# A conv-attention-MoE kernel on one core: twelve pipeline passes written out instead of looped, Newton steps of both norms on GpSimd, and x loaded earlier

## The chip, the cores and the metric

One core of a Trainium2 chip runs the whole kernel. The time is the device time in microseconds; a run of the kernel before takes 2311.79 us (median of three). In the profile PE is TensorE's matmul, PEld its weight load, DVE is VectorE, ACT is ScalarE, POOL is GpSimd and SP is SyncE, which only issues transfers.

## The reference, cut to what matters

The input x is (16, 16, 48, 128): 16 batches of 768 tokens with 128 channels. Three layers follow one another, each added to its input:

```
x = x + attention0(groupnorm(x))        # 8 heads of 16, relative biases, causal in t
t = tokens(x)
t = t + additive_attention(layernorm(t))  # logits[i,j] = sum_h w2[h] * tanh(A[i,h] + B[j,h] + b1[h])
t = t + moe(layernorm(t))               # 8 experts, top 2 of a softmax gate, capacity 1920, gelu
```

Both layernorms and the groupnorm are (v - mean) / sqrt(var + 1e-5). The additive attention needs 768 x 768 x 16 values of tanh per batch, the largest single piece of work on ACT.

## The kernel before, in words

**Passes, stages, ticks.** The first two layers and the gate run as a software pipeline over the batches. A pass has 24 ticks; in it five batches are worked on at once, each in another stage: "pre" (groupnorm, q, k, v), "max" (the maxima of the scores), "mid" (scores, softmax, heads, projection, first layernorm, the maps A, B and V), "add" (the additive attention, one group of sums and Tanh per tick) and "end" (the last block of that attention, second layernorm, gate, routing, sending the rows to the experts). Pass b has batch b+3 in "pre", b+2 in "max", b+1 in "mid", b in "add" and b-1 in "end". The first passes come in parts (the list `head`, up to pass 0), passes 1 to 12 are full and run in a loop on the engines (six iterations of two passes), passes 13 to 16 are the tail, and the experts follow (from about 2040 us on). Head and tail passes are written out in the program already.

**Order of work.** Each engine has its own program, made by the same Python function `body(ps)`; it walks over the ticks, and each tick has four slots on PE and DVE (`tick_order`). PE fills three PSUM banks in turn (`ring`), DVE reads them in the same order; PE's fill number n waits for DVE's read n-2. The table `AT` says in which tick a use of the ring stands. In the loop the counts that the waits ask for are worked out from the loop's register. Written-out passes have constants.

**Engines in one pass.** In each tick POOL writes three sums A + B into `hidden` (L837, one slot of four), ACT takes their Tanh (L956, a long one; L962, a fourth group with the sum in its bias), and PE adds them to the logits (L1037). POOL's sums of tick q wait for the logits of tick q-4. ACT also takes the Exp of the scores (L933) and, every fourth tick, of the logits (L940), which waits for a maximum that DVE takes (L1496). DVE takes the maxima of the first layer's scores (L1310) and copies most results out of the ring. POOL sends the rows to the experts too (L866).

**What the change touches.** On SP, `store_block` writes a finished block of `x2` to the output; `load_x` brings the next batch of "pre" into `x_in`, at tick 0 of a pass; the transposes xT of it stand at ticks 1 and 2. The store of block 4 of a pass is the last thing SP does in that pass. On DVE, `norm_scale(which, k)` works out 1/sqrt(var + eps) by a seed (L1194, k = 0) and three Newton steps (L1197, L1199, L1201, with a drain between operations). The second norm (which = 1) carries in its seventh column the groupnorm of the batch in "pre"; its four parts stand at `NORM_AT`, ticks 4 to 6. Its users are the normed rows of "end" (`normed`, L1266, tick 6, slots 1 and 3) and xnT (L1508, tick 7, slot 1). The first norm (which = 0) has only its seed on DVE; its steps run on POOL at tick 20 (L847 to L853). The products B, A and V of the transposed x1 (ticks 21 and 22, L1129 and L1111) wait for the copies of both halves of it.

## Time and profile before

| | before |
|---|---|
| median of 3 runs | 2311.79 us (2310.83 to 2315.6) |
| the profiled execution | 2323.02 us, its span 2321.2 us, mean granted clock 0.969 |
| busy | PE 2069.1 us (89%), ACT 1684.1 us (73%), DVE 1601.4 us (69%), POOL 1519.7 us (65%) |
| instructions with a place in the program | 59625 |

Instructions of a sequencer (register arithmetic, branches, waits, the issue of a transfer) don't count as busy. A row of a timeline gives start and length in us, engine, line, operation, tiles and count, and in brackets how long the engine had been idle and what released it. A pass is placed here from the long Tanh (L956) of its tick 0 to that of the next pass; pass 0 begins at 169.5 us, pass 1 at 274.1 us, pass 13 at 1717.7 us.

### The profile page before, as it was taken

Reading aid. Unit: us, or ns where it says so; the run is one execution under the profiler, and the core shown is the slowest. Engines: PE = TensorE matmul, PEld = TensorE weight load, DVE = VectorE, ACT = ScalarE, POOL = GpSimd, SP = SyncE. Lnnn points to the kernel's source line nnn. Section 1 sums busy time; section 2 is a strip of 40 time slices with the busy share of each in tenths; the row PEclk is TensorE's granted clock in tenths of the full one; section 3 lists DMA queues with packets and bytes.
Section 4 is the critical chain, followed back from the end, with each engine's and each line's share of the span. In section 5 each row is a group of like instructions: output and inputs, shape, how many; then the busy total and the mean of one; then the engine's idle time right before and its main releaser. Section 6 shows DMA issues by size and latency. Waiting matters only on the chain.

```text
span 2321.2 us, 59625 instructions
## 1 busy us (share of the span) xinstructions
PE 2069.1 (89%) x19525; PEld 1205.1 (52%) x19525; DVE 1601.4 (69%) x4309; ACT 1684.1 (73%) x1934; POOL 1519.7 (65%) x1735
## 2 busy tenths in 40 slices
PE   3889999999999999989998989999999978889996
PEld 2555555555554545455554545454555443458775
DVE  7787786868777777778786878686867554424443
ACT  4449887878887888878787888787888988624332
POOL 5117667576766667666767575757576878737777
PEclk7899999999999999999999999999999998999998
DMA  3746321322222323232323232313131000025553
GB/s 97 123 83 145 82 47 56 57 55 52 64 54 65 56 62 58 62 59 61 57 60 61 56 62 48 68 26 77 33 70 30 12 6 5 25 47 86 88 86 36
DMA packets 157506, 138.14 MB, mean 60 GB/s; under 512 B 24665, under 2 KB 149814, under 8 KB 157104
## 3 DMA queue, kind: packets, MB, share of 16 engines
q1 hardware_dynamic: 119376, 109.87, 22.9%
q0 software_dynamic: 23824, 16.85, 5.3%
q10 hardware_dynamic: 13968, 7.30, 1.3%
q8 instruction: 165, 2.70, 0.5%
q14 instruction: 173, 1.42, 0.2%
HBM read 82.68 MB, written 54.52 MB: 59 GB/s over the span
## 4 chain that ended last, share of the span: by engine, by line
PE 42%; DVE 18%; issue 13%; DVEq 9%; POOL 7%; POOLq 4%; ACT 3%; DMA 3%; SPq 2%; ACTq 0%
PE logits L1037 12%; POOL out_dram L590 4%; PE av_bank L1023 4%; PE ring L1137 4%; DVE max_halves L1310 4%; PE ring L1115 4%; PE scores L1007 3%; PE scores L1010 3%; PE ring L1129 3%; POOLq L836 2%; POOL hidden L837 2%; ACT hidden L956 2%; SPq L604 2%; PE ring L1134 1%; PE ring L1100 1%
## 5 line engine op out<-in xcount | busy, mean ns | idle before, releaser
L837 POOL TENSOR_SCALAR hidden<-b_rep,a_cols 128x768 f32<-128x768 f32 x1152 | 1054.9, 920 | 524.0 <-PE logits L1037 292.3
L956 ACT ACTIVATE hidden<-hidden 128x2304 f32<-128x2304 f32 x384 | 816.2, 2126 | 12.1 <-POOL hidden L837 12.1
L1037 PE MATMUL logits<-hidden,w_shifted 128*32 128x384 f32 x6144 | 586.5, 500 | 60.2 <-ACT probs L940 25.4
L933 ACT ACTIVATE probs<-scores 128x512 f32<-128x512 f32 (+1 forms) x768 | 394.4, 547 | 277.5 <-PE scores L1010 274.9
L1310 DVE TENSOR_REDUCE max_halves<-ring 128x4 f32<-128x512 f32 (+1 forms) x704 | 451.0, 659 | 117.6 <-PE ring L1115 117.2
L962 ACT ACTIVATE hidden<-b_rep,a_cols 128x768 f32<-128x768 f32 x384 | 358.5, 934 | 0.0
L1037 PEld LDWEIGHTS logits<-hidden,w_shifted 128*32 128x32 f32 x6144 | 163.2, 110 | 294.3 <-issue 237.7
L1115 PE MATMUL ring<-k_max,q_max 112*128 112x128 bf16 x2688 | 272.0, 224 | 15.4 <-DVE max_halves L1310 11.6
L1007 PE MATMUL scores<-bias_q,onehot_k 112*128 112x512 bf16 (+1 forms) x768 | 275.8, 360 | 4.1 <-DMA q_parts<-max_parts 2.2
L1010 PE MATMUL scores<-q_parts,k_parts 98*128 98x256 bf16 (+1 forms) x1536 | 277.1, 262 | 0.0
L1115 PEld LDWEIGHTS ring<-k_max,q_max 112*128 112x128 bf16 x2688 | 182.1, 99 | 157.4 <-issue 57.3
L866 POOL DMA_INDIRECT expert_rows<-rows,slots x198 | 201.7, 1019 | 59.2 <-issue 37.7
L1023 PE MATMUL av_bank<-probs,v_aug 128*32 128x256 f32 (+1 forms) x3072 | 223.0, 362 | 11.5 <-DVE headsT_raw L1482 10.5
L1010 PEld LDWEIGHTS scores<-q_parts,k_parts 98*128 98x128 bf16 x1536 | 153.1, 100 | 89.9 <-issue 18.5
L940 ACT ACTIVATE probs<-logits,logit_bias 128x768 f32<-128x768 f32 x96 | 86.6, 902 | 107.7 <-DVE logit_bias L1498 105.9
L517 ACT ACTIVATE hidden<-scores,eb1T 128x384 f32<-128x384 f32 x80 | 46.5, 581 | 162.8 <-PE scores L478 160.1
L1137 PE MATMUL ring<-v,probs1T 128*128 128x128 f32 x1152 | 151.2, 282 | 10.9 <-DVE max_halves L1310 9.2
L1137 PEld LDWEIGHTS ring<-v,probs1T 128*128 128x128 f32 x1152 | 138.9, 194 | 24.1 <-DVE max_halves L1310 18.5
L1368 DVE COPY probs1T<-ring 128x384 f32<-128x384 f32 x192 | 101.7, 550 | 43.7 <-PE ring L1134 43.6
L1007 PEld LDWEIGHTS scores<-bias_q,onehot_k 112*128 112x128 bf16 x768 | 78.0, 102 | 96.0 <-issue 65.4
L489 PEld LDWEIGHTS logits<-probs,hidden 128*128 128x128 f32 x960 | 113.4, 192 | 12.5 <-issue 2.2
L1023 PEld LDWEIGHTS av_bank<-probs,v_aug 128*32 128x32 f32 x3072 | 70.0, 108 | 87.7 <-issue 56.0
(272 smaller groups left out, 2665.1 us busy)
## 6 DMA issues: line engine op xcount, KB each, us to landing
qk_parts<-qk_parts_sb SPq DMA_DIRECT2D x16, 1152.0 KB, 4.5
q_parts<-qk_parts SPq DMA_DIRECT2D x192, 96.0 KB, 3.1
k_parts<-qk_parts SPq DMA_DIRECT2D x192, 96.0 KB, 4.1
q_max<-qk_parts SPq DMA_DIRECT2D x96, 96.0 KB
k_max<-qk_parts SPq DMA_DIRECT2D x96, 96.0 KB
expert_rows<-clear_row ACTq DMA_DIRECT2D x9, 792.0 KB, 5.4
x_in<-in_x_dram SPq DMA_DIRECT2D x96, 64.0 KB
x<-in_x_dram SPq DMA_DIRECT2D x96, 64.0 KB
```

Of the source, the lines that this page charges most:

```text
L837: last = g.tensor_scalar(hidden[:, q % SLOTS, o, :], b_rep[:, side], 1.0, a_cols[:, side, a_col(q, o):a_col(q, o) + 1], ALU.mult, ALU.add)
L866: pool.indirect_dma_start(rows_dram, bass.IndirectOffsetOnAxis(slots[:, k, tb:tb + 1], 0), rows[:, tb, :], None, bounds_check=E * CAP - 1, ...
L933: s.activation(probs0[:, d % 3, 2 * pair:2 * pair + 2, 0:n_], scores[:, pair].rearrange("p (j l) -> p j l", j=2)[:, :, 0:n_], ACT.Exp) \
L956: s.activation(hidden[:, t % SLOTS, 0:3, :], hidden[:, t % SLOTS, 0:3, :], ACT.Tanh)
L962: s.activation(hidden[:, t % SLOTS, 3, :], b_rep[:, side], ACT.Tanh, bias=a_cols[:, side, col:col + 1]).then_inc(tanh_done, 1)
L1007: mm(bank[:, :, 0:n_], onehot_k[:], bias_q[:, h:h + 2, q0 - P * kb:q0 - P * kb + n_], start=True, stop=False, skip_group_check=True)
L1010: last = mm(bank[:, j, 0:n_], k_parts[0:98, h + j, P * kb:P * kb + P], q_parts[0:98, h + j, q0:q0 + n_], start=False, stop=True, skip_grou ...
L1023: last = mm(av_bank[32 * g:32 * g + 32, q0 - lo:q0 - lo + n_], v_aug[:, side, kb, 4 * quad + g, :], probs0[:, d % 3, g, 0:n_], start=(kb = ...
L1037: last = mm(logits[32 * g:32 * g + 32, half, 0:HALF], w2_shifted[:, k, :], hidden[:, q % SLOTS, g, HALF * half:HALF * half + HALF], start= ...
L1115: last = mm(bank[:, P * j:P * j + P], q_max[:, h + j, P * qb:P * qb + P], k_max[:, h + j, P * kb:P * kb + P], start=True, stop=True)
L1137: last = mm(bank[:, 0:P], probs1T[:, P * kb:P * kb + P], v1[:, ps.side(stage), kb, :], start=(kb == 0), stop=(kb == TB - 1))
L1310: v.tensor_reduce(max_halves[:, h % 4:h % 4 + n_, BLOCK_PAIRS.index((qb, kb))], bank[:, 0:n_ * P].rearrange("p (h k) -> p h k", h=n_), AX. ...
```

## The change

The loop over passes 1 to 12 becomes twelve copies of the body, with constants in every wait and address. The Newton steps of the second norm move to POOL at tick 6, as those of the first were at tick 20: DVE makes the seed at tick 4 and signals, POOL does twelve small operations and signals back, DVE waits for that before the normed rows (now slots 2 and 3 of tick 6) and before xnT. Where a pass has "pre" and no "mid", the steps stay on DVE. On SP the store of block 4 goes from the end of its pass to tick 1 of the next, behind the load of x. The first half of A, B and V waits for the copy of the first half of x1T alone.

```
@@ -101,7 +101,7 @@
 SPLIT_AT = ((14, 1), (16, 0))
 SEND_FROM, SENDS = 18, 12
 NORM_AT = ((4, 3), (5, 0), (5, 2), (6, 0))
-SCALE_AT = 20
+SCALE_AT = (20, 6)
 SPLIT = 18
 CLEAR_AT = tuple(range(1, 19, 2))
 CLEARS = 1 + len(CLEAR_AT)
@@ -195,10 +195,8 @@
             body(Pass(b, b % 2, stages, base, base % RING, ticks))
             if i == 0 and prepare:
                 prepare()
-        with eng.Fori(0, (last_full - first_full + 1) // 2) as two:
-            for odd in (1, 0):
-                done = two * 2 + (1 - odd)
-                body(Pass(done + first_full, odd, STAGES, done * per_pass + base_full, base_full % RING))
+        for done in range(last_full - first_full + 1):
+            body(Pass(done + first_full, (done + 1) % 2, STAGES, done * per_pass + base_full, base_full % RING))
         base = base_full + (last_full - first_full + 1) * per_pass
         for b in range(last_full + 1, NB + 1):
             body(Pass(b, b % 2, stages_of(b), base, base % RING))
@@ -338,8 +336,8 @@
         av_copied = sem("av_copied")
         res_loaded = sem("res_loaded")
         x1n_ready = sem("x1n_ready")
-        x1_seeded = sem("x1_seeded")
-        x1_scaled = sem("x1_scaled")
+        norm_seeded = [sem(f"norm_seeded_{which}") for which in range(2)]
+        norm_scaled = [sem(f"norm_scaled_{which}") for which in range(2)]
         ab_ready = sem("ab_ready")
         sums_ready = sem("sums_ready")
         tanh_done = sem("tanh_done")
@@ -636,10 +634,10 @@
                 sp.dma_start(k_max[48:96, :, :], ct_wide).then_inc(copies_in, 16)
                 sp.dma_start(k_max[96:112, :, :], cn_wide).then_inc(copies_in, 16)
 
-            def store_block(ps, stage, s):
+            def store_block(ps, stage, s, read):
                 b = ps.batch(stage)
 
-                sp.wait_ge(ring_read, ps.number((stage, "attended", s)) + 1)
+                sp.wait_ge(ring_read, read)
                 sp.sem_inc(sp_passed, 1)
 
                 if positive(count := b * 96 + 16 * s):
@@ -709,17 +707,15 @@
                                 load_max(c, 0)
                         if t == SPLIT and positive(c):
                             load_max(c, 0)
-                    if ps.has("end") and t == 4:
-                        store_block(ps, "end", 5)
+                    if ps.has("end") and t in (1, 4):
+                        store_block(ps, "end", 4 + t // 4, ps.base if t == 1 else ps.number(("end", "attended", 5)) + 1)
                     if ps.has("mid") and t == 7:
                         c = ps.batch("mid")
                         for tb in range(TB):
                             sp.dma_start(x1[:, ps.side("mid"), tb, :], x[c, :, 8 * tb:8 * tb + 8, :]) \
                               .then_inc(res_loaded, 16)
                     if ps.has("add") and t >= 8 and t % 4 == 0:
-                        store_block(ps, "add", t // 4 - 2)
-                if ps.has("add"):
-                    store_block(ps, "add", 4)
+                        store_block(ps, "add", t // 4 - 2, ps.number(("add", "attended", t // 4 - 2)) + 1)
 
             passes(sp, body)
             expert_loads(sp)
@@ -838,10 +834,10 @@
                                            a_cols[:, side, a_col(q, o):a_col(q, o) + 1], ALU.mult, ALU.add)
                 last.then_inc(sums_ready, 1)
 
-            def norm_scale(ps):
-
-                var, y, tmp = (ln_small[:, 0, r, 0:TB] for r in range(3))
-                pool.wait_ge(x1_seeded, ps.batch("mid") + 1)
+            def norm_scale(which, c):
+
+                var, y, tmp = (ln_small[:, which, r, 0:TB + which] for r in range(3))
+                pool.wait_ge(norm_seeded[which], c + 1)
                 pool.sem_inc(pool_passed, 1)
                 for step in range(3):
                     g.tensor_tensor(tmp, y, y, ALU.mult)
@@ -852,7 +848,7 @@
                     pool.drain()
                     last = g.tensor_tensor(y, y, tmp, ALU.mult)
                     if step == 2:
-                        last.then_inc(x1_scaled, 1)
+                        last.then_inc(norm_scaled[which], 1)
                     else:
                         pool.drain()
 
@@ -870,8 +866,10 @@
                 for t in ps.ticks:
                     if ps.has("add"):
                         sums(ps, t)
-                    if t == SCALE_AT and ps.has("mid"):
-                        norm_scale(ps)
+                    if t == SCALE_AT[0] and ps.has("mid"):
+                        norm_scale(0, ps.batch("mid"))
+                    if t == SCALE_AT[1] and (ps.has("mid") or ps.has("end")):
+                        norm_scale(1, ps.batch("pre") - 2)
                     if ps.has("end"):
                         here = sends(ps)
                         if t < TICKS - SEND_FROM:
@@ -1078,7 +1076,7 @@
                 elif name == "x1T":
                     pe.wait_ge(x1n_ready, c + 1)
                 elif name in ("A", "B", "V"):
-                    after("x1T", 1)
+                    after("x1T", i)
                 elif name == "probsT":
                     pe.wait_ge(probs1_ready, c * 6 + (i[0] + 1))
                 elif name == "attended":
@@ -1190,17 +1188,6 @@
         def _(dve):
             v = nc.vector
 
-            def rsqrt_seed(y, var):
-                return v.tensor_scalar(y.bitcast(I32), var.bitcast(I32), -0.5, float(0x5F3759DF), ALU.mult, ALU.add)
-
-            def rsqrt_step(y, var, tmp):
-                v.scalar_tensor_tensor(tmp, y, -0.5, y, ALU.mult, ALU.mult)
-                dve.drain()
-                v.tensor_tensor(tmp, tmp, var, ALU.mult)
-                dve.drain()
-                v.scalar_tensor_tensor(y, tmp, 1.5, y, ALU.add, ALU.mult)
-
-
             def signal():
                 dve.drain()
                 v.memset(flag[:, 1:2], 0.0).then_inc(setup_dve, 1)
@@ -1249,18 +1236,28 @@
                 dve.drain()
                 v.bn_aggr(ln_mv[:, which, tb, :], ln_stats[:, which, tb, :])
 
-            def norm_scale(which, k):
-                n_ = TB + which
-                var, y, tmp = (ln_small[:, which, r, 0:n_] for r in range(3))
-                dve.drain()
+            def rsqrt_seed(which):
+                var, y = (ln_small[:, which, r, 0:TB + which] for r in range(2))
+                dve.drain()
+                v.tensor_scalar(var[:, 0:TB], ln_mv[:, which, :, 1], 1e-5, None, ALU.add)
+                dve.drain()
+                return v.tensor_scalar(y.bitcast(I32), var.bitcast(I32), -0.5, float(0x5F3759DF), ALU.mult, ALU.add)
+
+            def norm_seed(which):
+                rsqrt_seed(which).then_inc(norm_seeded[which], 1)
+
+            def norm_step(which, k):
+
                 if k == 0:
-                    v.tensor_scalar(var[:, 0:TB], ln_mv[:, which, :, 1], 1e-5, None, ALU.add)
-                    dve.drain()
-                    last = rsqrt_seed(y, var)
-                    if which == 0:
-                        last.then_inc(x1_seeded, 1)
-                else:
-                    rsqrt_step(y, var, tmp)
+                    rsqrt_seed(which)
+                    return
+                var, y, tmp = (ln_small[:, which, r, 0:TB + which] for r in range(3))
+                dve.drain()
+                v.scalar_tensor_tensor(tmp, y, -0.5, y, ALU.mult, ALU.mult)
+                dve.drain()
+                v.tensor_tensor(tmp, tmp, var, ALU.mult)
+                dve.drain()
+                v.scalar_tensor_tensor(y, tmp, 1.5, y, ALU.add, ALU.mult)
 
             def normed(which, src, dst, tb):
                 return v.tensor_scalar(dst[:, tb, 0:P], src[:, tb, :], ln_mv[:, which, tb, 0:1],
@@ -1497,23 +1494,26 @@
                             dve.drain()
                             v.tensor_scalar(logit_bias[:, 1:2], logit_bias[:, 0:1], b2_col[:], b2_col[:], ALU.subtract,
                                             ALU.add).then_inc(max1_ready, 1)
-                        if ps.has("pre") or ps.has("end"):
-                            if (t, slot) in NORM_AT:
-                                norm_scale(1, NORM_AT.index((t, slot)))
+                        if (ps.has("mid") or ps.has("end")) and t == 4 and slot == 3:
+                            norm_seed(1)
+                        elif ps.has("pre") and not ps.has("mid") and (t, slot) in NORM_AT:
+                            norm_step(1, NORM_AT.index((t, slot)))
                         for w, (at, first) in enumerate(SPLIT_AT):
                             if ps.has("pre") and t == at and first <= slot < first + 3:
                                 split(w, slot - first, ps.batch("pre"))
                         if ps.has("pre") and t == 7 and slot == 1:
                             dve.drain()
+                            if ps.has("mid"):
+                                dve.wait_ge(norm_scaled[1], ps.batch("pre") - 1)
                             v.tensor_scalar(xnT[:], xT[:], gn_small[:, 0:1], ln_small[:, 1, 1, TB:TB + 1], ALU.subtract,
                                             ALU.mult).then_inc(xn_ready, 1)
                         if ps.has("end"):
                             c = ps.batch("end")
-                            if t == 6 and slot in (1, 3):
-                                if slot == 1:
-                                    dve.drain()
+                            if t == 6 and slot in (2, 3):
+                                if slot == 2:
+                                    dve.wait_ge(norm_scaled[1], ps.batch("pre") - 1)
                                     dve.wait_ge(rows_sent, 112 + c * 192)
-                                for tb in range(3 * (slot // 2), 3 * (slot // 2) + 3):
+                                for tb in range(3 * (slot - 2), 3 * (slot - 2) + 3):
                                     last = normed(1, x2, rows, tb)
                                 if slot == 3:
                                     last.then_inc(x2n_ready, 1)
@@ -1545,11 +1545,11 @@
                                 for tb in range(half.start, half.stop):
                                     v.bn_aggr(ln_mv[:, 0, tb, :], ln_stats[:, 0, tb, :])
                             if t == 17 and slot == 2:
-                                norm_scale(0, 0)
+                                norm_seed(0)
                             if (t, slot) in ((19, 1), (19, 3)):
                                 half = slice(0, 3) if (t, slot) == (19, 1) else slice(3, 6)
                                 if half.start == 0:
-                                    dve.wait_ge(x1_scaled, ps.batch("mid") + 1)
+                                    dve.wait_ge(norm_scaled[0], ps.batch("mid") + 1)
                                 for tb in range(half.start, half.stop):
                                     last = normed(0, x1_, x1n, tb)
                                 if half.start:
```

## Rows read from the trace of the kernel before

**Rows 1.** The page: its span, and the chain that ended last, by engine.
```profile
span 2321.2 us, 59625 instructions
...
PE 42%; DVE 18%; issue 13%; DVEq 9%; POOL 7%; POOLq 4%; ACT 3%; DMA 3%; SPq 2%; ACTq 0%
```

**Rows 2.** Windows by pass: passes 0, 1, 6 and 13 (time, busy us and count, clock).
```profile
core 0: us, PE busy (x) PEld busy (x) DVE busy (x) ACT busy (x) POOL busy (x), PEclk, DMA share, GB/s
169.50:274.10 104.60, 100.22 (x1042) 55.65 (x1046) 79.73 (x185) 94.74 (x107) 71.57 (x88) 1.00 0.51 118
274.10:395.10 121.00, 112.11 (x1128) 62.35 (x1124) 92.78 (x241) 97.25 (x111) 80.97 (x97) 0.97 0.26 55
875.70:993.40 117.70, 108.87 (x1125) 61.17 (x1120) 91.42 (x241) 97.44 (x110) 80.54 (x96) 1.00 0.28 59
...
1717.70:1830.00 112.30, 102.45 (x1080) 56.96 (x1073) 81.66 (x210) 96.00 (x111) 79.57 (x96) 1.00 0.21 35
```

**Rows 3.** Timeline of ACT, ticks 0 and 1 of pass 5, tick 1 of pass 6.
```profile
755.13 2.12 ACT L956 ACTIVATE hidden<-hidden 128x2304 f32<-128x2304 f32 x1
...
765.73 2.11 ACT L956 ACTIVATE hidden<-hidden 128x2304 f32<-128x2304 f32 x1
...
882.75 2.12 ACT L956 ACTIVATE hidden<-hidden 128x2304 f32<-128x2304 f32 x1
```

**Rows 4.** Waits by engine and line (us in total, times, longest), DVE's first copy.
```profile
DVE headsT_raw L1482 <- issue: 15.1, 5, 3.1
```

**Rows 5.** Pass 4: SP's load of x, PE's first transposes; all such waits of L1100.
```profile
638.73 4.74 SPq L604 DMA_DIRECT2D x_in<-in_x_dram  x6
...
646.45 0.54 PE L1100 MATMUL ring<-ident,x_in 128*128 128x128 f32 x3 [2.18 <-DMA x_in<-in_x_dram]
...
  DMA x_in<-in_x_dram: 21.3, 11
```

**Rows 6.** Timeline of SP at tick 20 of pass 4: the store of block 3.
```profile
739.50 0.64 SPq L648 DMA_DIRECT2D out_dram<-x  x1
```

**Rows 7.** Timeline of DVE, ticks 4 to 6 of pass 5: seed, and the maximum of tick 6.
```profile
783.73 0.17 DVE L1194 TENSOR_SCALAR ln_small<-ln_small 128x7 int32<-128x7 int32 x1
...
790.04 0.68 DVE L1310 TENSOR_REDUCE max_halves<-ring 128x4 f32<-128x512 f32 x1
```

**Rows 8.** Timeline of PE, tick 7 of pass 5: transposes of the heads.
```profile
793.96 0.66 PE L1122 MATMUL ring<-ident,headsT_raw 128*128 128x128 f32 x4 [1.16 <-DVE probs1T L1368]
```

**Rows 9.** Pass 5: POOL's first sum for tick 7, and ACT's Tanh of tick 7.
```profile
782.68 0.91 POOL L837 TENSOR_SCALAR hidden<-b_rep,a_cols 128x768 f32<-128x768 f32 x1 [0.20 <-issue]
...
791.24 2.15 ACT L956 ACTIVATE hidden<-hidden 128x2304 f32<-128x2304 f32 x1
```

**Rows 10.** Timeline of POOL at tick 20 of pass 5: the Newton block's ends.
```profile
850.87 0.20 POOL L847 TENSOR_TENSOR ln_small<-ln_small 128x6 f32<-128x6 f32 x1
...
854.72 0.20 POOL L853 TENSOR_TENSOR ln_small<-ln_small 128x6 f32<-128x6 f32 x1
```

**Rows 11.** Pass 4, tick 20: first product of B; all such waits; a window there.
```profile
739.80 1.64 PE L1129 MATMUL ring<-headsT,map_b 128*128 128x384 f32 x2 [1.48 <-DVE headsT L1340]
...
PEld ring L1129 <- DVE headsT L1340: 25.7, 16, 1.7
...
739.60:743.00 3.40, 3.20 (x7) 1.61 (x8) 0.69 (x2) 3.28 (x5) 2.94 (x4) 0.51 0.08 21
```

**Rows 12.** Timeline of ACT: Tanh of tick 16 in pass 0 and in pass 6.
```profile
235.37 2.12 ACT L956 ACTIVATE hidden<-hidden 128x2304 f32<-128x2304 f32 x1
...
954.90 2.12 ACT L956 ACTIVATE hidden<-hidden 128x2304 f32<-128x2304 f32 x1
```

**Rows 13.** Pass 15: a Tanh of ACT. Pass 16: DVE's Newton steps, first and last.
```profile
1944.08 2.12 ACT L956 ACTIVATE hidden<-hidden 128x2304 f32<-128x2304 f32 x1 [1.21 <-POOL hidden L837]
...
2025.52 0.17 DVE L1197 SCALAR_TENSOR_TENSOR ln_small<-ln_small 128x7 f32<-128x7 f32 x1
...
2027.46 0.17 DVE L1201 SCALAR_TENSOR_TENSOR ln_small<-ln_small 128x7 f32<-128x7 f32 x1
```

## The prediction

> **What bounds the kernel now.** I read the page first, for the span and the busy shares, then the table of windows by pass, then the timelines of single ticks. The profiled execution has a span of 2321.2 us and took 2323.02 us with what lies around it, 11.2 us over the median of the runs, 2311.79 us (the table of times). The sum below is made against the span [rows 1], and its difference is then taken off the median. The chain that ended last is a mixture, PE 42%, DVE 18%, "issue" 13%, DVE's queue 9%, POOL 7% [rows 1]. So no engine bounds alone: a stall of any of them counts only where the others have no lead.
>
> A pass is 24 ticks. I place a tick at the start of its long Tanh on ACT (L956). The twelve passes of the loop lie between 274.1 and 1717.7 us, 120.3 us each; pass 0, written out but without stage "end", takes 104.6 us, and pass 13, written out without "pre", 112.3 us [rows 2]. ACT is busy 97.44 of the 117.7 us of pass 6 [rows 2]: in most ticks it runs Tanh and Exp back to back, and nothing is won there by a faster DVE or PE. What can be won lies in the 20 us in which it waits, at the ticks in which an "end" or "mid" step holds PE and DVE up (0, 4, 7, 8, 12, 16, 20 to 22).
>
> **The change part by part.** *The jump back* (term 1). Five times DVE stands still in front of its first copy of a pass with nothing to wait for, 15.1 us in all, 3.1 us the longest [rows 4]. Tick 0 of pass 5, which follows a jump, takes 765.73 - 755.13 = 10.6 us; that of pass 6, which doesn't, 882.75 - 875.70 = 7.05 us [rows 2, 3]. There are five jumps (six iterations), which fits the five holes; passes 3, 5, 7, 9 and 11 carry them. Written out, no engine jumps: 5 x 3.4 us = -17 us. Cover for it: none, ACT idles through it.
>
> *x first* (term 2). The program order on SP puts the store of block 4 ahead of the load of x, and that store waits for the last DVE result of the pass. In pass 4 SP issues x at 638.73 us for 4.74 us, and the transposes of xT start at 646.45 us after 2.18 us in which PE waits for the landing [rows 5]. In that position PE holds up the logits. There are 11 such waits, 21.3 us in all [rows 5], most of them in the six even passes; behind a jump SP has caught up with PE, so with the jumps gone they would come in the odd passes too, and the two terms are won together. ACT has the Tanh of a tick ahead of it when PE stands there, so I count less than half of the waits. After the change SP passes from the store of block 3, issued at 739.50 us [rows 6], to x with nothing open: parts_ready for that x was reached at tick 17. Six issues of about 0.8 us end near 745 us, 15 us before PE wants them. The store of block 4 moves behind them to tick 1; its wait is for uses of the pass before, long read, and the next write of that block comes 22 ticks later. -9 us. Bounds: 0 (other waits take the place) and -21 us (nothing covers them).
>
> *The Newton steps of the second norm* (term 3). They are nine small operations on DVE with a drain before each, between the seed at 783.73 us and the maximum of tick 6 at 790.04 us, with two maxima and a copy mixed in: 6.1 us less about 1.8 us of these, 4.3 us of DVE [rows 7]. Who waits: DVE takes the maximum of tick 6 only at 790.04 us, copies probs1T late behind it, and PE stands 1.16 us at 793.96 us for that copy (it must free a bank) [rows 7, 8]. The normed rows now come behind that copy, not in front of it, so the copy can be done by 791.2 us, and PE is bound by its own order. -1.2 us per pass in ticks 7 and 8, where PE is the late engine (ACT then waits for PE scores). Not -4.3 us, since ticks 5 and 6 are ACT's.
>
> *What POOL gives for it.* The block of 12 operations with drains lasts 4.06 us, from 850.87 to 854.92 us [rows 10], and it now stands at tick 6 too, between sums(6) and sums(7); the first operation of sums(7) began at 782.68 us [rows 9]. The seed is there only at 783.73 + 0.17 = 783.90 us [rows 7]. So: seed 783.9 + 0.2 for the signal + 4.06 = 788.2; then sums(7), three operations of 0.91 us with a drain each, 3.2 us with the drains, ready at 791.4 to 791.6 us. ACT wants them at 791.24 us [rows 9]: it comes 0.2 to 0.4 us late, in a tick behind which ACT waits for PE anyway. Queued behind the block on POOL are sums(7) and all later ones; ACT waits for these. DVE needs the result at slot 2 of tick 6, no earlier than 791.2 us, so 3 us after it is there. I take the stall at nothing; if PE weren't late in tick 8 it would cost 0.4 us x 12 = 5 us. Passes 0 and 13 gain like the loop's: 14 x 1.2 = -17 us. Bounds: 0 and -2.4 us per pass (the second when the attended product of tick 7 comes forward as well).
>
> *Registers* (term 4). In the loop each wait's count is worked out from the loop's register. In ticks 16 to 23 pass 0 (no registers) takes 274.1 - 235.37 = 38.7 us and pass 6 (registers) 993.4 - 954.90 = 38.5 us [rows 2, 12]: no price at all in a third of the pass. For the rest there is only a bound: pass 6 is 13.1 us longer than pass 0, PE's work in it 8.65 us and DVE's 11.7 us more [rows 2], so 1.4 to 4.5 us are not explained by stage "end". I take 0.5 us, near the stretch where it could be measured: -6 us; ends 0 and -4.5 x 12 = -54 us, the latter only if "end" had no waits of its own.
>
> *The products of x1T* (term 5). B, A and V of half 0 now wait for the copy of half 0 alone. In pass 4 PE stood 1.48 us in front of the first product of B [rows 11]; and there are 16 such waits with 25.7 us in all; the second of the two copies is a third of that, some 0.5 us. 15 passes in reach: -7 us. Behind the stall the granted clock in 739.6 to 743.0 us was 0.51 (1.2 GHz) [rows 11]. Pass 1, which has no jump before it, has a mean clock of 0.97 and 121.0 us, where pass 6 has 1.00 and 117.7 us [rows 2]; four passes are of its kind. With waits for x in the difference too I put the clock at 2 of its 3.3 us, 8 us for the four, and count half of it gone, -4 us, since the stall is only shortened. The Trainium skill ("TensorE: Matmul & The Clock Gate", Part 1: The HAM clock gate) says that idling is PE's throttled default and activity releases it. By that rule alone all four stretches would go with the idle time, -8 us in place of -4; the trace agrees in so far as the stretch shown lies right behind a wait of PE.
>
> *The tail* (term 6). In pass 15 POOL is the bound: ACT waits 1.21 us for POOL's sums at 1944.08 us, and so at its neighbours [rows 13]. There the block of 4.06 us lies open: +4 us (bounds 2 and 5). In pass 16 nothing else runs: the steps take 2025.52 to 2027.63 us on DVE [rows 13], 2.1 us; on POOL 4.06 us and two signals: +2.3 us. Together +6 us. SPLIT, the sends and the expert stage stay as they are.
>
> Sum: -17 - 9 - 17 - 6 - 7 - 4 + 6 = -54 us on the span. 2311.8 - 54 = 2258 us.
>
> **The rivals.** *A. More comes back than I count* (registers and DVE's freed time pass on to PE in ticks 12 to 15). For it: PE waits for DVE in these ticks too, and the 1.4 to 4.5 us above. Against it: ticks 16 to 23. At 3 us a pass more, 2258 - 36 = 2222 us. *B. The Newton move gives nothing*, because POOL makes ACT late by what DVE saves (POOL's lead at tick 7 is 0), and x and the half waits give half: -17 - 5 - 0 - 3 - 4 + 6 = -23, 2289 us. For it: the seed stands on DVE behind a maximum and slips with it. *C. It gets slower: POOL's block lies whole in ACT's way* at tick 7. Place: the wait of POOL for the seed. If the seed came 4 us later against ACT than now, each of 16 passes would lose 4 us: +64 against -37 for the rest, 2339 us. It decides from a loss of 2.3 us a pass on, that is a seed at 786.2 us where now it is 783.9 us. Against it: seed and Exp of the same tick both hang on the same DVE, so they slip together. *D. The written-out program doesn't do what it says*: stalls of the loop's end come back as stalls of fetching code that is met for the first time. Against it: passes 0 and 13 are such code, and DVE has no 3 us hole in them. The time then is 2311.8 - 54 + 17 and up, 2275 us for as many stalls as now and no change from some 16 of them on. The Trainium skill ("Advanced Engine Details and Errata", ISA Cache) gives the sequencer two lines of 256 instructions; by it a loop of two passes never stays in the cache, and code met once costs what the loop costs now between its jumps, which speaks against D.
>
> **How the numbers follow.** The forecast, 2235 to 2280 us, 0.60; A 0.14 (2205 to 2235 us); B 0.15 (2280 to 2305 us); D as no change 0.03; C 0.06, with 0.02 for slower by other ways. The range leaves out the outer part of A and the part of B and all of D and C beyond it: 2225 to 2292 us. About 0.2% is what a measurement of this kernel can tell from no change (runs from 2310.83 to 2315.6 us). Faster 0.90, same 0.03, slower 0.07.
>
> **What would show it.** Right: no idle of 3 us on DVE at any pass's end, tick 0 near 7 us throughout; x on SP directly behind the store of block 3, and no wait of PE for x_in; passes of 115 to 117 us; 34 blocks (16 of the first norm, 18 of the second) of 12 small operations on POOL, 4.06 us each; PE's stall at the transposes of tick 7 gone; ACT waiting for POOL less than 1 us at tick 7; pass 15 some 4 us longer. Wrong: ACT waiting 2 us or more for hidden at tick 7 (C), DVE standing at norm_scaled[1], holes in all engines at regular distances (D), or passes under 114 us (A).

## The result: 2278 us, inside the range, at two thirds of the gain forecast

Four runs of the changed kernel gave a median of 2278.15 us (2273.98 to 2279.62), four of the kernel before on the same chip 2313.69 us. The ratio is 0.9844, interval 0.9825 to 0.9864: 1.6% faster, 36 us. Forecast were 2258 us and -54 us. In a later group of runs, on a chip that gave the kernel before 2321.89 us, the changed kernel took 2285.51 us, again 0.9843 (0.9813 to 0.9873). So kernels of different groups are compared below by their ratio to the kernel before on the same chip.

The page of the changed kernel, against [rows 1]: the span, and the chain that ended last by engine and by line.

```profile
span 2272.2 us, 54398 instructions
...
PE 26%; POOL 19%; issue 17%; DVE 15%; POOLq 13%; DVEq 5%; ACT 3%; DMA 2%; SPq 0%; ACTq 0%
POOL hidden L833 14%; POOLq L832 10%; PE logits L1035 7%; POOL out_dram L588 4%; DVE max_halves L1307 3%; PE av_bank L1021 3%; PE ring L1113 2%; PE scores L1005 2%; PE scores L1008 2%; PE ring L1135 2%; ACT hidden L954 1%; PE ring L1104 1%; ACT hidden L960 1%; PE ring L1127 1%; DVEq L1389 1%
```

POOL and its queue were 11% of the chain before [rows 1] and are 32% now. L832 is the drain ahead of POOL's products, L833 the products. This is what the forecast had not counted. The windows of passes 0, 1, 6 and 13, against [rows 2]:

```profile
163.50:268.00 104.50, 100.31 (x1046) 55.81 (x1046) 76.34 (x176) 94.91 (x107) 74.45 (x100) 1.00 0.52 123
268.00:383.90 115.90, 108.83 (x1128) 61.42 (x1121) 89.98 (x232) 96.69 (x111) 82.67 (x108) 1.00 0.28 57
847.60:963.30 115.70, 108.81 (x1127) 61.48 (x1123) 89.77 (x232) 96.66 (x110) 83.52 (x109) 1.00 0.29 60
1659.00:1769.60 110.60, 102.68 (x1080) 56.95 (x1073) 78.23 (x201) 95.72 (x110) 82.48 (x108) 1.00 0.21 36
```

Passes 1 to 12 take 115.9 us in the mean in place of 120.3, pass 13 110.6 in place of 112.3; pass 0 is the same, so the 1.2 us that the prediction counted for it did not come. Twelve passes give 52 us, more than the 36 of the medians: the profiled execution of the kernel before was slower than all four of its timed runs (2323.02 us), that of the changed kernel was its fastest run (2273.98). Gains read between these two traces are therefore on the high side. Taking each tick from one long Tanh to the next, as the prediction does, the means over passes 1 to 12 are as follows (us; all columns but "before" and "changed" are experiments, explained below; the last row is pass 15 alone, up to its last Tanh):

| stretch | before | loop only | steps on DVE | changed | double block | loads late | loads late, steps on DVE | sends late |
|---|---|---|---|---|---|---|---|---|
| tick 0 | 8.5 | 7.1 | 7.1 | 7.1 | 7.1 | 7.1 | 7.1 | 7.0 |
| tick 2 | 4.6 | 3.8 | 3.8 | 3.8 | 3.8 | 3.8 | 3.8 | 3.8 |
| ticks 3, 4 | 10.9 | 10.2 | 10.2 | 10.2 | 10.2 | 10.2 | 10.2 | 10.2 |
| tick 6 | 3.8 | 3.8 | 3.8 | 6.5 | 10.7 | 4.2 | 3.8 | 4.1 |
| ticks 7, 8 | 12.2 | 12.3 | 12.3 | 8.6 | 8.7 | 10.4 | 10.8 | 10.4 |
| ticks 20 to 22 | 17.1 | 17.0 | 15.9 | 16.2 | 16.3 | 16.1 | 16.1 | 19.7 |
| pass | 120.3 | 117.5 | 116.5 | 115.9 | 120.4 | 115.0 | 115.0 | 118.6 |
| pass 15 | 83.7 | 83.8 | 83.3 | 86.6 | 92.4 | 87.8 | 82.7 | 81.2 |

SP now issues the x of pass 5 right behind the store of block 3, still in pass 4, as forecast (against [rows 5, 6]):

```profile
719.64 0.61 SPq L646 DMA_DIRECT2D out_dram<-x  x1
720.36 4.30 SPq L602 DMA_DIRECT2D x_in<-in_x_dram  x6
```

ACT in pass 6, the Tanh of tick 4 and of tick 7 (what it waited for is in brackets):

```profile
867.67 2.12 ACT L954 ACTIVATE hidden<-hidden 128x2304 f32<-128x2304 f32 x1 [1.81 <-POOL hidden L833]
...
883.45 2.14 ACT L954 ACTIVATE hidden<-hidden 128x2304 f32<-128x2304 f32 x1 [3.18 <-POOL hidden L833]
```

POOL in the same stretch: products (L833) behind two long holes, then the first and the last operation of the Newton block, then the first product for tick 7:

```profile
858.43 0.91 POOL L833 TENSOR_SCALAR hidden<-b_rep,a_cols 128x768 f32<-128x768 f32 x1 [2.21 <-issue]
...
866.72 0.91 POOL L833 TENSOR_SCALAR hidden<-b_rep,a_cols 128x768 f32<-128x768 f32 x1 [4.38 <-issue]
...
875.92 0.21 POOL L843 TENSOR_TENSOR ln_small<-ln_small 128x7 f32<-128x7 f32 x1
...
879.84 0.20 POOL L849 TENSOR_TENSOR ln_small<-ln_small 128x7 f32<-128x7 f32 x1
880.24 0.97 POOL L833 TENSOR_SCALAR hidden<-b_rep,a_cols 128x768 f32<-128x768 f32 x1 [0.20 <-issue]
```

The block lasts 4.12 us, about as in [rows 10], but it begins the moment the product before it ends. It doesn't wait for the seed; POOL is late by itself, and the block lies whole in ACT's way. The waits of the changed kernel (us in total, times, longest), and under them the one of the kernel before that answers to the second:

```profile
POOL hidden L833 <- issue: 234.8, 701, 5.0
...
ACT hidden L954 <- POOL hidden L833: 66.0, 42, 4.4
```

```profile
ACT hidden L956 <- POOL hidden L837: 12.1, 13, 1.9
```

This was the sign that the prediction named for its rival C: ACT waiting 2 us or more for hidden at tick 7. It came true in 10 of the 12 passes (2.6 us in the mean of all 12). The kernel is still 1.6% faster: ticks 7 and 8 gave back 3.6 us for the 2.7 that tick 6 lost, and the rest of the change brought its own gain.

### The profile page after: what moved, and what is told of

It is laid out like the page before. It is cut to its first block, busy times and chain, and to the rows that moved or that the text cites. A ratio compares the mean times of both kernels' runs of the same rounds, so it can differ in the third digit from the quotient of the medians.

```text
span 2272.2 us, 54398 instructions
## 1 busy us (share of the span) xinstructions
PE 2061.4 (91%) x19525; PEld 1206.4 (53%) x19525; DVE 1550.8 (68%) x4147; ACT 1676.9 (74%) x1934; POOL 1565.4 (69%) x1951
## 4 chain that ended last, share of the span: by engine, by line
PE 26%; POOL 19%; issue 17%; DVE 15%; POOLq 13%; DVEq 5%; ACT 3%; DMA 2%; SPq 0%; ACTq 0%
POOL hidden L833 14%; POOLq L832 10%; PE logits L1035 7%; POOL out_dram L588 4%; DVE max_halves L1307 3%; PE av_bank L1021 3%; PE ring L1113 2%; PE scores L1005 2%; PE scores L1008 2%; PE ring L1135 2%; ACT hidden L954 1%; PE ring L1104 1%; ACT hidden L960 1%; PE ring L1127 1%; DVEq L1389 1%
## 5 line engine op out<-in xcount | busy, mean ns | idle before, releaser
L833 POOL TENSOR_SCALAR hidden<-b_rep,a_cols 128x768 f32<-128x768 f32 x1152 | 1054.7, 919 | 403.1 <-issue 234.8
L1035 PE MATMUL logits<-hidden,w_shifted 128*32 128x384 f32 x6144 | 582.8, 497 | 61.0 <-ACT hidden L960 29.9
L1035 PEld LDWEIGHTS logits<-hidden,w_shifted 128*32 128x32 f32 x6144 | 163.9, 110 | 294.2 <-issue 233.6
L862 POOL DMA_INDIRECT expert_rows<-rows,slots x198 | 202.4, 1022 | 55.7 <-issue 35.3
L1135 PE MATMUL ring<-v,probs1T 128*128 128x128 f32 x1152 | 151.1, 282 | 15.1 <-DVE max_halves L1307 12.9
L487 PEld LDWEIGHTS logits<-probs,hidden 128*128 128x128 f32 x960 | 113.4, 192 | 12.3 <-issue 2.0
L487 PE MATMUL logits<-probs,hidden 128*128 128x128 f32 x960 | 113.7, 275 | 1.9 <-DVE gn_small L557 1.9
```

The lines of the kernel that those rows point to most:

```text
L833: last = g.tensor_scalar(hidden[:, q % SLOTS, o, :], b_rep[:, side], 1.0, a_cols[:, side, a_col(q, o):a_col(q, o) + 1], ALU.mult, ALU.add)
L1035: last = mm(logits[32 * g:32 * g + 32, half, 0:HALF], w2_shifted[:, k, :], hidden[:, q % SLOTS, g, HALF * half:HALF * half + HALF], start= ...
L1135: last = mm(bank[:, 0:P], probs1T[:, P * kb:P * kb + P], v1[:, ps.side(stage), kb, :], start=(kb == 0), stop=(kb == TB - 1))
```

## The experiments

There are twelve runs in three groups of four: eleven other kernels, and the changed one again. The first group ran on one chip, the second and third on another. All of them compute the reference's result; experiment 3 takes more Newton steps than that needs. "..." marks cut code.

**1. The Newton steps on VectorE again** (the rows stay in slots 2 and 3)

```
-                    if t == SCALE_AT[1] and (ps.has("mid") or ps.has("end")):
-                        norm_scale(1, ps.batch("pre") - 2)
...
-                        if (ps.has("mid") or ps.has("end")) and t == 4 and slot == 3:
-                            norm_seed(1)
-                        elif ps.has("pre") and not ps.has("mid") and (t, slot) in NORM_AT:
+                        if (ps.has("pre") or ps.has("end")) and (t, slot) in NORM_AT:
...
```

> The changed kernel, but the Newton steps of the second norm on VectorE again, and its normed rows still written in slots 2 and 3 of tick 6. It computes all of the reference. Theory 1: the move was worth little. The changed kernel's ScalarE waits some 3 us for GpSimd's hidden product at tick 7 of each pass, since GpSimd's block of 4.1 us now stands ahead of it; with the block gone that wait goes (tick 6 back from 6.5 to 3.8 us), while ticks 7 and 8 take back their 0.7 and 2.9 us. Net about +1 us in each of 12 to 14 passes, so 2285 to 2295. Rival (GpSimd makes ScalarE late and the move costs more than it gives): as fast or faster than the changed kernel, 2265 to 2278. Rival (the move is worth the 1.2 us and more that were forecast): 2295 or more.

Measured: 2281.56 us against 2323.23, ratio 0.9809 (0.9776 to 0.9842). Against the changed kernel's 0.9843 that is as fast or faster; the intervals overlap. The ticks came as theory 1 has them: tick 6 3.8 us, ticks 7 and 8 12.3, a pass 0.6 us longer. But pass 15 is 3.3 us shorter. The time itself lies between the two ranges; put on the first chip by its ratio it is 2269 us, in the range of the first rival. So that rival fits the time, and theory 1 the passes.

**2. The loop written out and nothing else**

```
-        with eng.Fori(0, (last_full - first_full + 1) // 2) as two:
+        for done in range(last_full - first_full + 1):
...
```

> The kernel before with its loop written out over the twelve passes on every engine, and nothing else. It computes all of the reference. Theory: 5 jumps back of 3.4 us and some half a us of registers in each pass go, 23 us in all, of which the changed kernel's ticks 0 show 1.4 us in the mean of 12 passes (17 us): 2313.7 less 17 to 23, so 2290 to 2297. Rival: written-out code brings fetch stalls, and it is the same as before (2305 to 2315). Rival: the loop's registers cost more than the jump, and nearly all that the change gave comes from here: 2275 to 2283.

Measured: 2296.40 us, ratio 0.9881 (0.9839 to 0.9923), -27 us (18 to 37 by the interval). That is the theory's size or somewhat more, short of the second rival's 31 to 39; code met for the first time brought no stalls like those of the jumps. Its waits for x_in at PE's transposes are

```profile
PE ring L1098 <- DMA x_in<-in_x_dram: 6.9, 2, 6.6
```

where there were 21.3 us in 11 [rows 5]; 6.6 of these 6.9 us are one wait, which the changed kernel has as well. Tick 2 is at 3.8 us in all written-out kernels. So the wait for x went with the jumps.

**3. A Newton block twice as long on GpSimd**

```
-                for step in range(3):
+                for step in range(3 if which == 0 else 6):
...
```

> The changed kernel with six Newton steps instead of three in the second norm's block on GpSimd, which makes that block some 4 us longer (it computes more steps than the reference asks for). Theory 1: GpSimd's queue is what ScalarE waits for at tick 7, so nearly all of the added time comes out in each of 13 to 14 full passes: +45 to +60 us on the changed kernel, tick 6 from 6.5 to some 10 us, and the wait for hidden at tick 7 from 3 to 6 or 7 us. Rival: the block is covered and the wait has another cause: +15 us or less.

Measured: 2364.95 us, ratio 1.0164 (1.0113 to 1.0214), by ratio 74 us over the changed kernel; its profiled span is 2363.1 us, 90.9 over. Both are more than expected. A pass is 4.5 us longer in the mean of passes 1 to 12 (54 us together), 4.2 of it in tick 6; passes 0, 13, 14 and 15 add 4 to 6 us each, and the start and the stretch behind the last Tanh 7 and 10. In pass 6 ACT waits

```profile
919.85 2.12 ACT L954 ACTIVATE hidden<-hidden 128x2304 f32<-128x2304 f32 x1 [6.61 <-POOL hidden L833]
```

where it waited 3.18 us. Nothing covers the block: all that is put on GpSimd there comes out again. The rival falls.

**4. The loads of scores at tick 6, not 2**

```
                             load_max(c, 1)
+                        if t == 6:
                             load_scores(c, 0)
...
```

> The changed kernel with SyncE's loads of the next batch's scores issued from tick 6 on instead of tick 2. It computes all of the reference. Theory 2: this burst keeps the DMA engines full at ticks 0 to 4, where GpSimd stops behind its own indirect sends (the two holes of 2.3 and 4.2 us in each pass). With the burst later the holes are gone or move behind tick 7, GpSimd is ahead again at tick 6, the wait for hidden there falls from 3 us to under 1, and the time by 15 to 35 us, to 2243 to 2263. Rival: GpSimd stops for its sends whatever SyncE loads: holes and time stay, 2270 to 2285. Rival: the loads are then late for the next pass's scores: slower, 2285 or more.

Measured: 2276.97 us, ratio 0.9787 (0.9754 to 0.9820), some 13 us better than the changed kernel by ratio, though the time itself (2276.97) lies where the first rival put it; a pass is 0.9 us shorter. The mechanism came as expected, the gain was smaller than the 15 to 35 us expected. Windows of the same stretch (4 to 19 us behind the start of pass 6) in the changed kernel and in this one; the last three columns are clock, DMA share and GB/s:

```profile
851.60:866.70 15.10, 14.63 (x167) 8.57 (x165) 11.76 (x25) 13.19 (x16) 7.89 (x9) 1.00 0.87 132
```

```profile
851.10:866.20 15.10, 14.64 (x167) 8.57 (x166) 11.93 (x23) 14.01 (x17) 11.74 (x14) 1.00 0.31 58
```

With the DMA engines 87% busy POOL works 7.89 of 15.1 us, with 31% it works 11.74. Of its two holes one of 2 us is left. Then POOL does stand waiting for the seed; in pass 5 the block begins 0.2 us behind the seed and ends at 762.28 us:

```profile
758.17 0.20 POOL L844 TENSOR_TENSOR ln_small<-ln_small 128x7 f32<-128x7 f32 x1 [2.25 <-DVE ln_small L1245]
...
762.08 0.20 POOL L850 TENSOR_TENSOR ln_small<-ln_small 128x7 f32<-128x7 f32 x1
```

This is the order that the prediction had taken for the change itself (seed, signal, 4.1 us, then a product 0.2 to 0.4 us late), and tick 6 is 0.4 us over 3.8, just so.

**5. All sends late**

```
-                    return SENDS // 2 if ps.has("mid") else SENDS // 4
+                    return SENDS if ps.has("mid") else SENDS // 4
...
```

The ranges of the sends and the counts that wait for them are changed to match.

> The changed kernel with all twelve of GpSimd's indirect sends of a batch in ticks 18 to 23 of a pass and none in ticks 0 to 5. It computes all of the reference. With the loads of scores put at tick 6 instead, GpSimd's two long stops in ticks 0 to 5 went, tick 6 fell from 6.5 to 4.2 us, but tick 8 grew from 4.8 to 6.6 and the time stayed: so theory 1 now has a second half, that behind GpSimd's wait stands the chain over TensorE and VectorE of ticks 6 to 8, which ends some half a us later. By it this run shows tick 6 at 3.8 to 4.5 us, ticks 6 to 8 together 14.2 to 14.7 in place of 15.1, and 2265 to 2277 us. Rival (the sends are what keeps GpSimd from being ahead, and freeing it shortens each pass by the 2 us of tick 6): 2245 to 2260. Rival (six sends more in ticks 18 to 23 delay the gather of the next rows): 2282 or more.

Measured: 2310.68 us, ratio 0.9970 (0.9953 to 0.9987), 29 us slower than the changed kernel by ratio. The theory held for ticks 6 to 8 (14.6 us), but the time went where the second rival put it: ticks 20 to 22 take 19.7 us for 16.2, with a mean granted clock of 0.83 to 0.91 there in 11 of 12 passes (the changed kernel has 1.00 in 11 of 12). There POOL now makes two sends (L862) between products:

```profile
963.26 0.91 POOL L833 TENSOR_SCALAR hidden<-b_rep,a_cols 128x768 f32<-128x768 f32 x1 [0.34 <-issue]
964.32 1.01 POOL L862 DMA_INDIRECT expert_rows<-rows,slots  x1 [0.15 <-issue]
965.63 0.97 POOL L862 DMA_INDIRECT expert_rows<-rows,slots  x1 [0.30 <-issue]
```

and ACT waits 3.11 us for DVE's bias at tick 20, where the changed kernel waits 1.51:

```profile
965.34 0.90 ACT L938 ACTIVATE probs<-logits,logit_bias 128x768 f32<-128x768 f32 x1 [3.11 <-DVE logit_bias L1495]
```

What holds DVE up at tick 20 is one instruction. Of the six normed rows of the first norm (L1263, `heads`) one takes 2.4 to 2.6 us in each of the twelve passes, where the longest takes 0.85 in the changed kernel (1.05 once). Here it is in pass 6, with what POOL does meanwhile, and then the same row in the changed kernel:

```profile
960.50 2.50 DVE L1263 TENSOR_SCALAR heads<-x,ln_mv,ln_small 128x128 f32<-128x128 f32 x1
```

```profile
960.11 0.97 POOL L862 DMA_INDIRECT expert_rows<-rows,slots  x1 [0.30 <-issue]
961.12 1.79 POOL L833 TENSOR_SCALAR hidden<-b_rep,a_cols 128x768 f32<-128x768 f32 x2
```

```profile
945.88 0.85 DVE L1263 TENSOR_SCALAR heads<-x,ln_mv,ln_small 128x128 f32<-128x128 f32 x1
```

The row starts inside the second send and ends 0.1 us after the two products behind it. ACT's wait for the bias grows by about as much, from 1.7 to 3.4 us in the mean. So the second rival's time came by another way than the gather that it named.

The holes of POOL in ticks 0 to 5 are gone here with the loads at tick 2. So the long hole needs both: a send of POOL's, and a burst of SP's beside it.

**6. x late again**

```
-                    if ps.has("end") and t in (1, 4):
-                        store_block(ps, "end", 4 + t // 4, ps.base if t == 1 else ps.number(("end", "attended", 5)) + 1)
+                    if ps.has("end") and t == 4:
+                        store_block(ps, "end", 5, ps.number(("end", "attended", 5)) + 1)
...
+                if ps.has("add"):
+                    store_block(ps, "add", 4, ps.number(("add", "attended", 4)) + 1)
```

> The changed kernel with the store of block 4 at the pass's end again, so that the load of x stands behind it as before. It computes all of the reference. Theory (forecast -9 for x first; TensorE stood 0.8 us at tick 2 in the mean of 12 passes before): tick 2 back to 4.6 us, 2278 + 5 to 10, so 2283 to 2288. Rival (written out, the descriptors go out 3 us earlier at each pass's start, so x is in time in either order): 2272 to 2281, no wait at tick 2.

Measured: 2280.98 us, ratio 0.9846 (0.9808 to 0.9884); the mean pass is 116.0 us for 115.9, tick 2 3.8 us, and pass 13 alone is 5.3 us longer. Pass 13 can't be put down to the order: the changed kernel has 110.6 us there in its first profile and 114.2 in its second (experiment 9). The rival holds: once the loop is written out the order is worth 0 to 3 us, less than these runs can tell from nothing.

**7. The whole wait for x1T**

```
-                    after("x1T", i)
+                    after("x1T", 1)
```

> The changed kernel where TensorE waits for the whole of x1T before its transposes again instead of for one half at a time. It computes all of the reference. Theory (forecast -7 for the half waits): some half a us more in each pass and a few stretches at the lower clock back, 2283 to 2290. Rival: another wait ends last there and it is the same, 2274 to 2281.

Measured: 2283.89 us, ratio 0.9879 (0.9828 to 0.9930). That is 3 us over experiment 6 on the same chip and 8 over the changed kernel by ratio, but the intervals overlap; the traces have to decide. PE's waits in front of B, first here, then in the changed kernel:

```profile
PE ring L1127 <- DVE headsT L1337: 21.0, 16, 1.7
```

```profile
PE ring L1127 <- DVE headsT L1337: 13.7, 15, 1.3
```

Each is 0.4 to 0.5 us longer, a pass 0.6 us, and ticks 20 to 22 0.5 us. The theory fits.

**8. Sends and loads late** (the edits of experiments 4 and 5 together)

> The changed kernel with both: loads of scores from tick 6 and all sends of a batch in ticks 18 to 23. It computes all of the reference. By theory 1 with its second half, GpSimd is ahead at tick 6 and the chain over TensorE and VectorE sets ticks 6 to 8 at 14.2 to 14.6 us, as with the late loads alone: 2265 to 2277. Rival (the two add up): 2255 or less. Rival (loads and sends now meet late in the pass, or GpSimd's sends delay the gather): 2282 or more.

Measured: 2308.83 us, ratio 0.9968 (0.9946 to 0.9990); ticks 6 to 8 at 14.6 us, ticks 20 to 22 19.8. The second rival's time again, as in experiment 5: behind GpSimd's lateness the floor of ticks 6 to 8 is 14.6 us, whichever of the two is moved.

**9. The changed kernel again**

> The changed kernel as it is, run beside the three kernels that follow so that they have it on the same chip. Every theory: 2274 to 2280 us. One thing more is looked at. In three of the written-out kernels (steps on VectorE, loop written out only, loads late) VectorE stood 6.1, 8.9 and 4.7 + 5.4 us at the end of pass 15 with its inputs ready; in the changed kernel's profile it didn't. If that stall is drawn anew in each execution this profile may show it; if it belongs to the program's layout it does not.

Measured: 2285.51 us, ratio 0.9843 (0.9813 to 0.9873), above the expected 2274 to 2280 on a chip on which the kernel before is slower too. Its profile shows the stall that the first one didn't have: VectorE at the end of pass 15, where PE's last product of the logits (L1035) had ended at 1965.0 us:

```profile
1963.53 1.50 PE L1035 MATMUL logits<-hidden,w_shifted 128*32 128x384 f32 x16
```

```profile
1965.73 0.18 DVE L1237 BATCH_NORM_AGGREGATE ln_mv<-ln_stats 128x2 f32<-128x6 f32 x1
1972.03 0.96 DVE L1493 TENSOR_REDUCE logit_bias<-logits 128x1 f32<-128x768 f32 x1 [6.12 <-remote]
```

The program is the same, so the stall doesn't belong to its layout.

**10. Loads late, VectorE's program shifted by 100 places**

```
             v = nc.vector
+            for _ in range(100):
+                dve.drain()
```

> The kernel with the loads of scores from tick 6, with 100 drains put at the very start of VectorE's program, where it waits for data anyway, so that every later instruction of VectorE lies 100 places further on. It computes all of the reference. Theory 3: the stall of some 10 us of VectorE at the end of pass 15 comes from where in the code VectorE is at that moment (fetching instructions behind the expert weights' transfers), so it moves or goes: 2266 to 2271, last Tanh to the end 316 to 319 us in place of 324.5. Rival: the stall belongs to a wait of the kernel and stays at its place: 2274 to 2278.

Measured: 2286.68 us, ratio 0.9848 (0.9819 to 0.9877). Both expectations missed. The drains were not covered: the first Tanh of pass 0 comes at 176.6 us, 10.5 us later than with late loads alone. And the stall is there, 6.1 us, in front of the same maximum of the logits as in experiment 9, 13.2 us behind the start of the last long Tanh in both. So theory 3, as put, falls: the stall doesn't hang on the place in VectorE's code. What causes it stays open.

**11. Loads late, the steps of passes 15 and 16 on VectorE**

```
-                    if t == SCALE_AT[1] and (ps.has("mid") or ps.has("end")):
+                    if t == SCALE_AT[1] and ps.has("mid"):
...
```

> The kernel with the loads of scores from tick 6, with the second norm's Newton steps on VectorE in passes 15 and 16 (GpSimd is late there) and on GpSimd in all passes before. It computes all of the reference. Theory 1: pass 15 goes back from 87.8 to some 83.5 us and pass 16 gives 2 to 3 us: 5 to 8 us under the kernel with late loads, 2268 to 2272. Rival: these blocks were covered there: 2275 to 2278.

Measured: 2266.16 us, ratio 0.9759 (0.9728 to 0.9790): pass 15 84.1 us for 87.8, the stretch behind the last Tanh 321.5 for 324.5. By ratio that is 6 us under experiment 4, within theory 1's 5 to 8; the ratios' intervals overlap, the two stretches show it.

**12. Loads late, the steps on VectorE everywhere** (the edits of experiments 1 and 4 together)

> The changed kernel with both: loads of scores from tick 6 and the second norm's Newton steps on VectorE in every pass. It computes all of the reference. Against the kernel with late loads alone it gives the worth of the move where GpSimd isn't late. By the forecast (1.2 us a pass in 14 passes less 6 in the tail) and the ticks 6 to 8 of the two kernels measured (16.1 with the steps on VectorE, 14.6 without): ticks 6 to 8 at 16.1 us, pass 15 back to 83.5 us, 2282 to 2290 without a stall of VectorE. Rival (VectorE was never the late one, and only GpSimd's queue counts): 2265 to 2275.

Measured: 2266.85 us, ratio 0.9768 (0.9739 to 0.9798). The rival holds. Passes 6 and 15:

```profile
843.80:958.50 114.70, 108.69 (x1124) 61.45 (x1120) 91.66 (x241) 96.98 (x110) 80.31 (x96) 1.00 0.29 61
1857.60:1940.30 82.70, 67.14 (x573) 30.40 (x572) 36.78 (x102) 72.51 (x60) 71.68 (x78) 0.94 0.03 6
```

The mean pass is 115.0 us, that of experiment 4 with the steps on GpSimd also 115.0, and ticks 6 to 8 take 14.6 us in both. Where GpSimd isn't late, the move is worth nothing in the loop, and experiment 4 against this one shows that it costs at the end: 5.1 us in pass 15. This kernel and that of experiment 11 take 18.7 and 19.4 us off the changed one, measured beside them.

## Why the forecast held, and which of its steps did not

**The jump back and the registers (terms 1 and 4, -23 us): right.** Tick 0 went from 8.5 to 7.1 us in the mean of 12 passes, 16 us, and DVE's five holes [rows 4] have no counterpart, so rival D fell. The loop alone gave 27 us by ratio. Its passes are 2.8 us shorter: 1.4 tick 0, 0.8 tick 2, 0.6 ticks 3 and 4. The last may be the registers, being of the size taken (0.5); no run parts them.

**x first (term 2, -9 us): the right sum at the wrong address.** The 0.8 us of tick 2 came, 9 us over 12 passes, but experiment 2 has them without the new order and experiment 6 keeps them without it. The prediction had expected the waits to move to the odd passes once the jumps were gone; they went.

**The half waits (term 5, -7 us): right by the traces,** 0.6 us a pass in experiment 7. The clock's -4 us can't be told apart: pass 1 has 1.00 where it had 0.97 [rows 2], and it has 1.00 with the loop written out alone too.

**The Newton steps (term 3, -17 us): this step failed.** It said that DVE is the late engine of ticks 7 and 8 and that 1.2 us a pass come back. Measured in the changed kernel against experiment 1: 0.6 us a pass, 7 us; with the loads late, nothing. DVE was not late by its own work alone. The wait that the prediction read, PE in front of the transposes of the heads [rows 8], is gone in experiment 1 without the move, probably by the new slots of the rows; ticks 7 and 8 didn't shorten (12.3 us), since PE now stands for the same copy a little later. PE's waits for it, first with the loop alone, then in experiment 1:

```profile
PE ring L1120 <- DVE probs1T L1366: 18.5, 12, 1.8
```

```profile
PE ring L1133 <- DVE probs1T L1363: 12.7, 16, 1.6
...
PE ring L1118 <- DVE probs1T L1363: 0.3, 1, 0.3
```

Pass 6 of experiment 1, POOL with its hole, then the seed and the first steps on DVE:

```profile
868.26 0.91 POOL L833 TENSOR_SCALAR hidden<-b_rep,a_cols 128x768 f32<-128x768 f32 x1 [4.11 <-issue]
```

```profile
874.84 0.81 DVE L1242 TENSOR_SCALAR ln_small<-ln_small 128x7 int32<-128x7 int32 x1
875.73 0.61 DVE L1254 SCALAR_TENSOR_TENSOR ln_small<-ln_small 128x7 f32<-128x7 f32 x1
...
887.31 0.41 DVE L1305 TENSOR_REDUCE max_halves<-ring 128x2 f32<-128x256 f32 x1
```

and the same three in experiment 12, whose pass 6 begins at 843.80 us (that of experiment 1 at 849.39):

```profile
868.80 0.72 DVE L1243 TENSOR_SCALAR ln_small<-ln_small 128x7 int32<-128x7 int32 x1
869.60 0.17 DVE L1255 SCALAR_TENSOR_TENSOR ln_small<-ln_small 128x7 f32<-128x7 f32 x1
...
879.67 0.41 DVE L1306 TENSOR_REDUCE max_halves<-ring 128x2 f32<-128x256 f32 x1
```

From the seed to the last maximum DVE takes 12.5 us with POOL late and 10.9 with POOL ahead (12.1 and 10.8 in the mean of passes 1 to 12), with the same instructions and the same idle time between them; what grows is single operations, the small ones from 0.17 us to 0.6 to 0.8. In ticks 7 and 8 ACT then waits 2.1 us for PE's scores in the mean, and 0.7 with POOL ahead. The two kernels differ in the place of the loads alone, so the loads set the end of these ticks in the layout with the steps on DVE too. There it shows as a slow DVE and a late PE in tick 8, with the steps on POOL as a late POOL at tick 7.

Why DVE's instructions grow can be read from where they end. Of the 120 DVE operations of 128x7 (seed and steps) in passes 1 to 12 of experiment 1, 57 take over 0.3 us, and 50 of these end within 0.03 us of the end of a product of POOL's; in experiment 12 it is 46, and all 46 end so. So they stand until POOL's product is through, in both kernels, and more often where POOL is catching up. No run took POOL's products away alone. The Trainium skill ("SBUF — State Buffer", SBUF: two separate sides) has a rule for it: VectorE and GpSimd share a pair of ports under an exclusive lock, and whichever comes second of a GpSimd operation and a VectorE operation that has two SBUF inputs, or runs in a two-port mode, stands still for the whole of the first. The 0.61 us of a step with two inputs in place of 0.17, and the common ends, agree with it. The seed has one input; whether it runs in such a mode, no run here shows.

**POOL's price, taken at nothing: this step failed too.** "ready at 791.4 to 791.6 us", 0.2 to 0.4 us late, took POOL's place in the old trace [rows 9] for its place in the new one. POOL's lead can be read off as the time from the end of its third product for tick 7 to the Tanh that reads it. In the mean of passes 1 to 12 it was 5.0 us before, and enough for the block. With the loop written out (experiment 2) it is 1.8 us (0.9 to 2.9). Of these 3.2 us some 1.8 a pass are holes of POOL's over 1 us, which grew from 79 to 100 us in the twelve passes; the rest fits the jumps and waits that went and had been POOL's slack, which is argued. In experiment 1, which has everything but the block, the lead is 1.4 us. A block of 4.1 us on a lead of 1.4 makes ACT 2.7 us late, and tick 6 grew by 2.7. Experiment 3 shows that the block is uncovered, experiment 4 why POOL is late: with the loads late and the steps on DVE (experiment 12) the lead is 5.8 us.

**The tail (term 6, +6 us): the right places, too small.** Pass 15 takes 3.3 us more than in experiment 1 (87.7 us in experiment 9: 4.4 more). In pass 16 DVE's rows wait for the block

```profile
1973.93 1.63 DVE L1263 TENSOR_SCALAR rows<-x,ln_mv,ln_small 128x128 f32<-128x128 f32 x6 [5.39 <-POOL ln_small L849]
```

for 5.39 us. From the last Tanh on experiment 9 takes 325.8 us, experiment 1, with the same stall of DVE, 319.5: 6.3 more, where 2.3 were forecast. Together 11 us, not 6.

**The sum.** Forecast were -54 us. Of these -32 were for the loop and x, measured -27 by experiment 2; -11 for the half waits and the clock, measured -3 to -8; -11 for the Newton steps with their tail, measured a loss instead: +4 by the parts above (-7 in the loop, +11 in the tail), +8 by the ratios 0.9809 without the move and 0.9843 with it (intervals that overlap), +10 by the spans of experiments 1 and 9. The parts add up to -20 to -31, the whole to -36. Experiment 1 stands 17 us below experiment 2 by ratio where the half waits explain at most 8; a part of what ticks 20 to 22 gave back (1.1 us a pass) and the slots of the rows were not tried alone and stay open.

The time fell near the slow end of the forecast's 2235 to 2280 us because the written-out loop carried it. For the Newton steps the mechanism was that of rival B (chance 0.15): POOL makes ACT late by what DVE saves. That the total still landed in the range is partly luck: the terms for the steps and their tail were wrong by 15 to 21 us, and 5 to 16 us that no term foresaw and no run explains made up for a part of it. (The chances of the prediction give slower 0.06 + 0.02; its last line has 0.07.)

## What to carry to other kernels

Before work is moved to an engine that "is ahead", look for what eats its lead in the stretch before it, above all a drain or a wait behind its own DMA issues, and work out its place in the new order, not in the old trace. An engine that waits less elsewhere leaves less slack to its neighbours: removing stalls of one kind can take the cover from work of another. And a late engine can show under another engine's name; delaying one burst of loads by four ticks was worth more here than the whole move of the Newton steps.

## What was not expected of the hardware

At the drains behind its indirect sends POOL stood 2.2 and 4.4 us in pass 6, in a stretch with the DMA engines 87% busy, and most of it went with SP's loads elsewhere (holes over 1 us in passes 1 to 12: 99 us against 44 in experiment 4). A VectorE instruction that met POOL's operations stood up to 2.6 us (experiment 5). And VectorE stood 6 to 10 us at one place, ending 7 to 13 us behind the start of the last long Tanh, in all eight profiles of the first and third group, and in none of the second, although the second ran on the same chip as the third; shifting its program by 100 instructions didn't move it. The kernel before took 10, 4 and 8 us more beside the three groups than at first (2323.23, 2317.62 and 2321.89 us against 2313.69), so it may have the stall too; no profile of it was taken there, and the cause is open.
